# One layer of split-head attention and a two-branch expert mixer on one core: the side products between the heads' blocks placed anew

## What is computed

```python
x = L0_attn_x                                    # (8, 1024, 256) f32
xn = _layernorm(x, axis=-1)
x = x + _L0_attn_ref(xn, ...) + _L0_ffn_ref(xn, ...)

# _L0_attn_ref: 16 heads of 16; heads 0..3 causal ("global"), heads 4..15 causal within 64 keys ("local")
qkv = x @ w_qkv + b_qkv
ctx_g = _attend(q[:, :NUM_GLOBAL], k[:, :NUM_GLOBAL], v[:, :NUM_GLOBAL], gmask)
ctx_l = _attend(q[:, NUM_GLOBAL:], k[:, NUM_GLOBAL:], v[:, NUM_GLOBAL:], lmask)
return ctx @ w_out + b_out

# _L0_ffn_ref: two branches (fwd, inv), 8 experts of width 64 each
xV = jnp.einsum('btd,kdr->btkr', Q_side, V)
yW = jnp.einsum('btd,kdr->btkr', K_side, W)
cum_yW = jnp.cumsum(yW, axis=1)
prod = xV * cum_yW
h = jax.nn.gelu(Q_side @ router_w1.T + router_b1, approximate=False)
weights = jax.nn.softmax(h @ router_w2.T + router_b2 + expert_bias, axis=-1)
out = jnp.einsum('btkr,kdr->btd', prod * weights[..., None], U) + weights @ b
out = out / n_valid[None, :, None]               # fwd + 0.5 * inv, then @ W_O.T
```

## Time and profile before

| | us |
|---|---|
| three runs of the kernel | 1486.11, 1491.48, 1492.9 |
| median | 1491.48 |
| the profiled execution | 1491.34 |
| its span, first to last instruction | 1489.6 |
| an even chunk without its predecessor's end (chunk 6) | 78.33 |
| an odd chunk (chunk 7) | 95.87 |
| chunk 0, chunk 5 | 89.88, 98.65 |

### The profile page before, as it was taken

The page is one execution under the profiler, slowest core; times in us unless marked ns, Lnnn a source line. Parts: engine busy times, 40 slices in busy tenths (PEclk is TensorE's granted clock), DMA queues, the critical chain, the costliest instruction groups (busy, mean ns, idle before and its releaser), DMA issues.

```text
span 1489.6 us, 35980 instructions
## 1 busy us (share of the span) xinstructions
PE 1379.5 (93%) x14481; PEld 1035.7 (70%) x14481; DVE 989.5 (66%) x2082; ACT 776.1 (52%) x1368; POOL 586.5 (39%) x663
## 2 busy tenths in 40 slices
PE   5978999999999999999999999999999999999996
PEld 4567685777758677586856778587775868667773
DVE  6667777567756777557875677566875578656661
ACT  2434537455464735645374554646356453755544
POOL 1025343453514444253433525144452534335341
PEclk9999999999999999999999999999999999999998
DMA  8430625326062541616353171624516153431610
GB/s 189 102 94 11 168 79 127 105 65 174 25 175 70 121 126 49 166 32 151 96 123 107 40 196 30 158 87 107 141 42 163 44 146 100 118 109 42 172 40 15
DMA packets 166614, 152.88 MB, mean 103 GB/s; under 512 B 37809, under 2 KB 149808, under 8 KB 166448
## 3 DMA queue, kind: packets, MB, share of 16 engines
q1 hardware_dynamic: 166448, 150.59, 38.8%
HBM read 108.57 MB, written 35.65 MB: 97 GB/s over the span
## 4 chain that ended last, share of the span: by engine, by line
PE 62%; DVE 15%; ACT 8%; issue 6%; DMA 4%; POOL 2%; SPq 1%; ACTq 0%; POOLq 0%; DVEq 0%
PE PS L676 30%; PE PS L787 11%; PE PS L821 4%; DVE rest L1193 3%; PE PS L880 3%; ACT HE L1063 3%; PE PS L807 3%; PE PS L909 3%; PE PS L898 2%; PE PS L963 2%; DMA weights_d<-weights_t 2%; DVE area L1198 2%; DVE area L1196 2%; ACT HE L1055 2%; ACT PS L1048 1%
## 5 line engine op out<-in xcount | busy, mean ns | idle before, releaser
L1504 POOL TENSOR_TENSOR PL<-prod,PH 128x512 fp32r<-128x512 f32 x128 | 164.7, 1287 | 201.3 <-ACT PH L1037 201.3
L676 PE MATMUL PS<-XH,WH 128*128 128x512 f32 x512 | 218.6, 427 | 21.7 <-ACT prod L1027 10.3
L1037 ACT ACTIVATE PH<-prod 128x512 fp32r<-128x512 f32 x128 | 80.8, 632 | 268.8 <-DVE prod L1305 252.8
L1499 POOL TENSOR_TENSOR prod<-prod,rest 128x512 f32<-128x512 f32 x96 | 124.8, 1303 | 242.9 <-DMA rest<-weights_d 166.6
L1229 DVE TENSOR_REDUCE block_peak<-PS 128x4 f32<-128x512 f32 x288 | 179.8, 685 | 48.0 <-PE PS L821 47.9
L676 PE MATMUL PS<-XH,WL 128*128 128x512 f32 x512 | 204.1, 399 | 0.0
L676 PE MATMUL PS<-XL,WH 128*128 128x512 f32 x512 | 203.6, 398 | 0.0
L1482 POOL TENSOR_SCALAR_AFFINE_SELECT HE<-HE 128x256 f32<-128x256 f32 x128 | 51.2, 406 | 364.2 <-ACT HE L1063 360.6
L1063 ACT ACTIVATE HE<-PS 128x512 f32<-128x512 f32 (+1 forms) x320 | 159.9, 553 | 33.5 <-PE PS L880 30.5
L1305 DVE TENSOR_TENSOR prod<-PS,prod 128x512 f32<-128x512 f32 x128 | 87.8, 686 | 97.3 <-PE PS L676 84.5
L676 PEld LDWEIGHTS PS<-XH,WH 128*128 128x128 f32 x512 | 97.1, 190 | 63.2 <-ACT prod L1027 16.8
(11 more groups left out here) (186 smaller groups left out, 3064.6 us busy)
## 6 DMA issues: line engine op xcount, KB each, us to landing
parts_d<-area SPq DMA_DIRECT2D x32, 768.0 KB, 5.0
area<-parts_d SPq DMA_DIRECT2D x128, 192.0 KB, 7.9
rest<-weights_d SPq DMA_DIRECT2D x192, 128.0 KB, 3.0
area<-parts_d SPq DMA_DIRECT2D x32, 576.0 KB, 7.8
tok<-in_L_attn_x_dram SPq DMA_DIRECT2D x16, 512.0 KB, 6.2
xt<-in_L_attn_x_dram SPq DMA_DIRECT2D x16, 512.0 KB, 4.1
wide<-weights_d SPq DMA_DIRECT2D x64, 128.0 KB, 3.0
out_dram<-xt SPq DMA_DIRECT2D x16, 512.0 KB, 3.8
```

Source lines behind the costliest of these rows:

```text
L676: ins = e.matmul(ps, a, b, start=first and k == 0, stop=last and k == n - 1, skip_group_check=True)
L1037: e.activation(PH[:, h, :], prod[:, j % 3, :], ACT.Copy).then_inc(phi)
L1499: e.tensor_tensor(prod[:, j % 3, :], prod[:, j % 3, :], wide[j % WIDE], ALU.mult).then_inc(weighed)
L1504: e.tensor_tensor(PL[:, j % 2, :], prod[:, j % 3, :], PH[:, j % 2, :].bitcast(F32), ALU.subtract).then_inc(plo)
```

## The change

The set of stages is the same; only their order is not.

- In the local heads both `turn` now stand in the first side group, and the last `mix` with both `sums` and the `rows` in the second; then the four `parts` follow, one in each group.
- In the global heads `gate_parts` stands one group earlier; `x` 1 and `x` 2 of the next chunk stand among the blocks (in an even chunk behind the second and the third `gav`, in an odd one behind the third and the sixth), `finish` 0 behind them (behind the fourth or the eighth `gav`), `values` 0 ahead of the last `gav` and `values` 1 behind it. The three first `weigh` stand together behind `chigh`.
- In chunk 0 `x` 1 is made ahead of the loop, the second chunk's `norm` follows the first four peaks in one piece, ahead of the first `product`, and the rest goes in the order of the other chunks. In chunk 15 the experts that were left for the local heads start one group earlier, and `finish` 0 stands in the middle of the global blocks, not behind the first.

```diff
@@ -258,7 +258,7 @@
 
         order = []
         for j in range(2 * KB):
-            if j < 2 * KB - 1 and (j > 1 or not ch):
+            if 1 < j < 2 * KB - 1:
                 order.append([(add_x, ch, j + 1, part) for part in range(2)] + [(add_weigh, ch, j + 1)])
             order.append([(add_c, ch, j, part) for part in range(2)] if j else [])
             order[-1].append((add_product, ch, j))
@@ -320,8 +320,6 @@
         gpeaks[2].append((add_rows, ch, 0))
         gpeaks[-1].append((add, "found", ch, 1))
         order += gpeaks
-        if ch == 0:
-            add_norm(1, order)
         blocks = range(0, len(order), PEAKS)
         joined = lambda groups, n: [stage for group in groups[n:n + PEAKS] for stage in group]
         return [joined(order, n) + joined(masks, n + PEAKS) for n in blocks]
@@ -379,6 +377,9 @@
     add_weigh(0, 0)
     for part in range(2):
         add_c(0, 0, part)
+    for part in range(2):
+        add_x(0, 1, part)
+    add_weigh(0, 1)
 
     for ch in range(CHUNKS):
         nxt = ch + 1 < CHUNKS
@@ -387,21 +388,28 @@
         split = len(experts) - (0 if nxt else 4)
         if ch:
             experts[1].append((add_finish, ch - 1, 1))
-            experts[2], experts[3] = experts[3], experts[2]
-        run(experts[0] + peaks[0])
+        experts[2], experts[3] = experts[3], experts[2]
+        if ch:
+            run(experts[0] + peaks[0])
+        else:
+            run(peaks[0])
+            for n in range(len(NORM)):
+                add("norm", 1, n)
+            run([(add_x, 0, 2, part) for part in range(2)] + [(add_weigh, 0, 2)] + experts[0])
         weave(experts[1:split], peaks[1:])
         if ch:
             add_residual(ch)
 
         last_mix = [(add_mix, ch, 2 * KB - 1, part) for part in range(2)]
         if nxt:
-            side = [[(add_turn, ch + 1, 0)], last_mix, [(add_turn, ch + 1, 1)], [(add, "sums", ch + 1, 0), (add_rows, ch, 1)]]
-            side += [[(add_parts, ch + 1, 1, 0), (add, "sums", ch + 1, 1)]]
-            side += [[(add_parts, ch + 1, w, b)] for w, b in ((1, 1), (0, 0), (0, 1))]
+            side = [[(add_turn, ch + 1, 0), (add_turn, ch + 1, 1)]]
+            side += [last_mix + [(add, "sums", ch + 1, 0), (add, "sums", ch + 1, 1), (add_rows, ch, 1)]]
+            side += [[(add_parts, ch + 1, w, b)] for w in (1, 0) for b in range(DB)]
             if ch + 2 < CHUNKS:
                 side[-1].append((add, "load", ch + 2))
         else:
-            side = [[(add_rows, ch, 1)]] + experts[split:] + [last_mix]
+            side = experts[split:] + [last_mix]
+            side[0] = side[0] + [(add_rows, ch, 1)]
         weave(local_groups(ch), side)
         add_lav(ch, NL // 4, 1)
         add("cturn", ch, 0)
@@ -414,33 +422,34 @@
                 add_hidden(ch + 1, j)
 
         order = global_groups(ch)
-        side = []
         if nxt:
-            first_x, first_c = ([(add, ch + 1, 0, part) for part in range(2)] for add in (add_x, add_c))
-            run(first_x + order[0] + first_c)
+            x0, x1, x2 = ([(add_x, ch + 1, j, part) for part in range(2)] for j in range(3))
+            run(x0 + order[0] + [(add_c, ch + 1, 0, part) for part in range(2)])
             add("logits", ch + 1, uses=["bank7"])
             add("chigh", ch, 0)
+            if ch + 2 < CHUNKS:
+                add_norm(ch + 2, order[1:])
+            steps = 2 + 3 * (ch % NC)
+            last = len(order) // 2 - 1
+
+            order[1] += [(add_gates, ch + 1), (add, "crest", ch, 0)]
+            for n, other in ((0, [(add_gate_parts, ch + 1)]), (steps // 2, x1), (steps, x2), (steps + steps // 2, [(add_finish, ch, 0)]),
+                             (last - 1, [(add_values, ch + 1, 0)])):
+                order[2 * n + 2] += other
             order = order[1:]
-            if ch + 2 < CHUNKS:
-                add_norm(ch + 2, order)
-            side = [[(add_gates, ch + 1)], [(add_gate_parts, ch + 1)]] + [[]] * (2 * (ch % NC))
-            side += [[(add_values, ch + 1, 0)], [(add_values, ch + 1, 1)]]
-            side[0].append((add, "crest", ch, 0))
         else:
             add("crest", ch, 0)
-        side.append([(add_finish, ch, 0)])
-        weave(order, side)
+            order[len(order) // 2].append((add_finish, ch, 0))
+        for group in order:
+            run(group)
         if nxt:
+            add_values(ch + 1, 1)
             add("stacks", ch + 1, "global")
-        if nxt:
-            add_weigh(ch + 1, 0)
-            run([(add_x, ch + 1, 1, part) for part in range(2)])
-            add_weigh(ch + 1, 1)
         add("cturn", ch, 1)
         add("chigh", ch, 1)
         if nxt:
-            run([(add_x, ch + 1, 2, part) for part in range(2)])
-            add_weigh(ch + 1, 2)
+            for j in range(WIDE):
+                add_weigh(ch + 1, j)
         add("crest", ch, 1)
     add_finish(CHUNKS - 1, 1)
```

## The result

The changed kernel takes 1508.9 us (median of four runs, 1505.95 to 1512.75) against 1488.8 (four runs, 1483.79 to 1492.9): a ratio of 1.0135, interval 1.0099 to 1.017. It is slower. The profiled execution took 1510.38 us, with a span of 1508.6 against 1489.6, so 19.0 us are to be explained.

A forecast was written before the change was run, and what follows sets the result against it. TensorE, 93% busy, was taken as the bound: its own list plus its waits. The terms +18 - 7 + 0 - 2 - 1 + 3 = +11, added to 1491.34, gave 1502 us, range 1478 to 1517.

The forecast's parts named there:

- the third rival: Local heads: the new wait brings the half clock in every second chunk, +22 in all, 1513 us; chance 0.14.
- the local heads: Third lav waits 2.1 us for GpSimd's select behind two sums; net +1.2 us per chunk, 15 times, +18.
- the odd ends: End of odd chunks: TensorE waits less, c 1 comes earlier; -1.0 us each, 7 times, -7 in all.
- the even ends: End of even chunks, 8 times: product stays where it was, VectorE coming last in place of the DMA; 0.
- chunk 0: c 1 comes 2.7 to 5 us later, but the wait at 129.37 and others go; -2 us, between -5 and +1.
- chunk 15: Experts fill the first waits in the local heads, the last group stands empty; -1 us, between -3 and +1.
- the clock: The new 2.1 us wait in the local heads brings two falls to half clock; +3 us, between 0 and +15.
- just enough: End of odd chunks: first product ready at 625.3 to 625.8, for c 1 at 625.6.
- The prediction's own sign: Odd chunks: c 1 starting more than 0.5 us from 3.7 behind the first lpeak would mean VectorE's chain is mis-sized.

The follow-up runs named there:

- e8: e5 with chunk 0 and chunk 15 in the order of the kernel before; 1484.47 us, ratio 0.9984 to the kernel before.
- e5: Changed kernel with the local heads' old side groups and GpSimd's second and third weigh waiting for crest; 1483.68 us, ratio 0.9976 to the kernel before.
- e3: Changed kernel with only the second sums moved behind the first parts, so the third selects stand between the sums; 1498.87 us, ratio 1.0066.
- e9: e3 with GpSimd's second and third weigh also waiting for crest, new local order otherwise kept; 1489.92 us, ratio 1.0014 to the kernel before.
- e2: Changed kernel with the local heads' side groups as they were before; 1491.5 us, ratio 1.0024 to the kernel before.
- e6: e5 with the normalization's last piece, the scaling of tok, behind the next chunk's first peaks; 1490.68 us, ratio 1.002 to the kernel before.

## Why the prediction was right, point by point

The time came out 6.9 us above the forecast of 1502, inside the range and on the predicted side, and 4 us below the third rival's 1513. The direction rests on the right mechanism; the sum is near only by luck, because errors of both signs met in it. In the order of the forecast's sum, the traces have +10.6 for the local heads (+18 forecast), -3.3 for the odd ends (-7), +6.4 for the even ends (0), -0.6 for chunk 0 (-2), -2.2 for chunk 15 (-1), and +12.4 for the clock (+3); less the 4.2 of the start these make the 19, where the forecast had 11. Against the median of 1488.8 the kernel lost 20 us, nearly twice the +11: part of the nearness is that the forecast was added to 1491.34.

**The local heads: right in kind, too large.** The `lav` was to start 10.7 to 10.9 us behind the first `lscore`; it started 10.53 behind it, after a wait of 1.65 in place of 2.1, since TensorE was ready 0.15 later and the `lav` could start 0.15 to 0.35 earlier than I had them. From there to the second `hidden` I expected 9.7 to 10.2 and the trace has 9.82. Net +0.74 in even chunks and +0.67 in odd ones with the full clock, in place of +1.2: 8 x 0.74 + 7 x 0.67 = 10.6 us where the sum had 18. The rest of the 15.2 is the half clock, three chunks (0, 5 and 6) with 1.5 each.

**The odd ends: right on TensorE, half of it lost on VectorE.** The last attention no longer waits, and the one before it waits 0.28 where I had 0.4. TensorE reached the first peak 1.04 us earlier, against the 1.0 of the sum. `c` 1 came only 0.48 earlier, 3.3 in all in place of 7, because the division of the context ran beside the third `weigh`. I had written that the first `product` would be ready "just enough"; what failed is that I took the chain on VectorE at its old durations, while the change puts three `weigh` in one piece next to it.

**The even ends: the term that failed.** Predicted 0, bounds -0.5 and +0.7; measured +0.8 each, 6.4 in all: +1.1 to +1.4 in five of them, +0.2 in three. The start of `crest` was right: 24.43 us behind the second `hidden` by the working (704.35 - 679.92), 24.66 in the trace. Its duration was not, 1.61 for 0.69, and 1.61 to 1.78 in four of the eight. (In chunk 8, +1.1, it took 1.06; there `c` 1 had come half a microsecond earlier than in chunk 6 before the change, and the later start of `crest` cost the rest.) The prediction's own sign for this, a `c` 1 of the odd chunks more than 0.5 us from 3.7 behind the first peak, came up in five of seven, with 4.6 to 4.9: the chain on VectorE was mis-sized. The prediction had the Trainium skill's rule on two SBUF inputs beside `sums` in the local heads, where it changed little (the division there took 1.31 before, at 668.48, and 1.30 now, at 316.96), and said that the sum didn't use it. It belonged here. The rows to see it were in the trace of before, between chunks 5 and 6, where `crest` took 1.16 beside a `weigh`, and I had not asked why:

```profile
622.51 1.29 POOL L1499 TENSOR_TENSOR prod<-prod,rest 128x512 f32<-128x512 f32 x1 [1.63 <-ACT prod L1027]
623.19 1.16 DVE L1338 TENSOR_TENSOR PL<-craw,PH 128x512 fp32r<-128x512 f32 x1 [0.70 <-ACT PH L1069]
```

In two even ends of that trace (chunks 8 and 12) `crest` even took 1.40 and 1.75, and cost nothing, with ends of 25.3 and 25.6 against 25.8 in chunk 6: it then began 1.4 us earlier. It is the later start, which the change makes, that takes this slack away.

**Chunk 0: the steps right, the gain not.** `c` 1 came 13.3 us behind the first peak, 5.2 later than before and after a wait of 8.98 (predicted 2.7 to 5 later, 6.7 or more), and the wait near 129 went. Together that was to give 2 us; it gave 0.6, and by e8 nothing. GpSimd ran three `weigh` in a row there, and of the small steps of the normalization beside them three took over a microsecond each, each up to the end of one `weigh`:

```profile
88.80 2.48 POOL L1508 TENSOR_TENSOR prod<-prod,rest 128x512 f32<-128x512 f32 x2 [69.81 <-DMA rest<-weights_d]
91.27 1.26 POOL L1508 TENSOR_TENSOR prod<-prod,wide 128x512 f32<-128x512 f32 x1
```

```profile
88.73 0.16 DVE L1164 TENSOR_TENSOR var<-var 128x4 f32<-128x4 f32 x1
88.93 1.15 DVE L1166 TENSOR_SCALAR var<-var 128x4 f32<-128x4 f32 x1
90.12 1.18 DVE L1168 TENSOR_TENSOR var<-var 128x4 f32<-128x4 f32 x1
91.33 1.22 DVE L1162 TENSOR_TENSOR var<-var 128x4 f32<-128x4 f32 x1
```

I had seen this as a possibility ("99 if GpSimd's three `weigh` hold up its small operations"); it cost about 3 us.

**Chunk 15.** -1 predicted, -2.2 in the trace, 0.9 between e8 and e5. The rest goes with the half clock: the kernel before had 3.4 us of it from 1438.9, 4 us behind that chunk's first `lscore`, and the changed kernel has none there. With the old order the last chunk took 49.7 to 50.9 in three traces, with the new one 48.6 to 49.8 in eight.

**The clock.** I took two falls for 3 us. There were many more: the half clock is in the local heads of chunks 0, 1, 5, 6, 7, 9, 11 and 13 and behind the late `c` 1 of six odd chunks. The latter cost most of the 7.8 us behind `c` 1 (38.8 to 40.3 for 37.6 to 37.7 in five of them; chunk 5 had it before, too), the former 4.6. That is the third rival's mechanism, but more than half of it hangs on the late `c` 1 and not on the wait in the local heads, of which the rival spoke. Not every fall costs: in the odd chunks 1, 7, 9, 11 and 13 it came about 5 us behind the first `lscore`, ahead of the wait, where it only took time that would have been waited, and these chunks took 21.23 us against 21.36 in chunk 3 without it. What sets off these early falls is open. They are in odd chunks of every kernel with the new local order, also in e3 and e9, where the wait behind them is gone and they cost 0.4 in five cases of six (21.0 for 20.6), and in none of the five with the old one (before, e2, e5, e6, e8). The Trainium skill, TensorE: Matmul & The Clock Gate, section HAM oscillation, says that gaps between bursts bring the throttle back. The traces agree in tendency: waits of 1.9 us at `c` 1 are followed by it in three of the four ends of e2 where `crest` was held up, and waits of 0.9 to 1.0 in e5 are not.

## What to carry to other kernels

When a change moves one engine's work next to another's critical steps, the durations of those steps are not constants: look in the old trace for the same operation at two durations and ask what ran beside the longer one. An order of side work that is right for TensorE can be undone by the list of a lightly loaded engine (GpSimd at 38% here); the cure was one wait on that engine, or one operation put between two others. And a wait of about 1.7 us on TensorE had to be priced here at up to twice its length, since the clock may fall behind it (1.5 us more).

## What was not expected of the hardware

- The collision is not bound to long operations: instructions of VectorE on 128x4 elements that take 0.16 to 0.17 us took 1.15 to 1.22 while `weigh` ran on GpSimd, and one of the three (L1166) has a single SBUF tensor as input. Nor is it bound to two inputs in the scaling of `tok`, 1.38 against 2.41.
- Whoever is first keeps the way. Where `crest` began first (703.15), it took 0.69 and the two `weigh` 2.84; where `weigh` was first, they took 2.49 and `crest` 1.61.
- The half clock ahead of a wait was free (21.23 us against 21.36); behind the wait, 3.4 us of it cost 1.5 us.
- Up to 5 us of difference between executions arise in the start alone, with the same instructions in it: 81.4 us without half clock there, 82.4 to 82.8 with 3.4 us of it, 85.3 to 86.9 with 10.2.
